# Where V is projected, when K is spread, and when a pair's weights are copied, in an attention and expert kernel

## The chip, the cores and the metric

The kernel runs on one core of a Trainium2 chip. The metric is the time of one execution on the device in microseconds (us). Lower is better.

## The reference

64 sequences of 64 tokens with 256 features (4096 tokens) pass through four steps; everything is fp32.

```python
c  = x @ cond_weight[id] + cond_bias[id]           # per sequence, one of 16 matrices
q, k, v, o projections: c @ W.T + b + c @ A.T @ B.T / 8      # 16 heads of 16
scores = q @ k.T / 4 + slope[h] * (key - query)
x  = x + (c + rezero * o_projection(softmax(scores) @ v))
y  = lora_out[lang](x) + lang_embed[lang]          # rank 16, one of 4 languages
x  = x + geglu(y @ Ws1 + bs1) @ Ws2 + bs2          # shared
       + sum over the top 2 of 12 experts of gate * (geglu(y @ We1 + be1) @ We2 + be2)
```

y has rank 16 in each of 4 languages. So the kernel never forms y: it multiplies the language matrices into the first layers ("merge") and feeds these with the low-rank rows.

## The kernel before

The tokens are cut into 32 tiles of 128 (two sequences each). The order of work is written out by hand for each engine. Engines meet through semaphores: an instruction ends with `then_inc(name)`, another engine executes `wait_ge(name, count)` and everything queued behind that on this engine waits too. Three stages follow each other.

**Attention, tiles 0 to 31 (to about 336 us).** In its tile step i TensorE does, in this order: score(i), c_transpose(i+1), inverse_transpose(i-1), low_rank(i-2) (rank-16 rows of a finished tile), project_k and project_q (i+1), output(i-1), the transpose of the probabilities prob_transpose(i), row_transpose(i-2), x2_transpose(i-1), project_v(i+1), condition(i+2), and last attend(i). VectorE does shift(i) (maximum and subtraction in two halves, with normalize(i-1) between them), k_spread(i+1), t_mask(i-2), x2_add(i-1), half of the copy of the transposed probabilities (pT_copy), sums(i), v_spread(i+1), invert(i), logit_sum(i-2), lang_part(i-1), c_add(i+2). ScalarE copies cT (L564), applies exp to both halves (L577), adds q's bias (L569), and copies transposes. GpSimd adds residuals and cuts merged biases into three bf16 parts.

[...] The scores take columns 0 to 255 of banks 0 to 3, and K and V of the next tile share bank 4: K in columns 0 to 255, V in 256 to 511. [...]

**Merging.** Tiles 1 and 2 merge the shared layer's weights. Tiles 3 to 7 merge nothing. From tile 8 on each expert takes two tiles. The even tile has merge_pair: the weights of two units into bank 6 (merge_weights, L1328), then attend, then their biases into bank 7 (merge_biases, L1334); only behind the biases does merge_ps rise. ScalarE copies the biases at once (pair_bias_copy, L556), and the weights in the odd tile behind the copies of cT and of the inverses (pair_copy, L559). The odd tile merges one unit (merge). low_rank needs bank 6, and so waits for pair_copy (merge_sb); in the odd tile (`after_pair`) it therefore runs behind project_q, in all other tiles ahead of project_k.

**Start.** VectorE adds the low-rank products to the weights of K, Q and V (low_rank_weight, L748) as they land by DMA, with c_add(0), the scaling of two biases, k_spread(0), v_spread(0) and c_add(1) between. SyncE issues the loads; ali_f (the alibi rows) raises the same semaphore as two biases (d_near). Behind tile 0, VectorE does router_consts, lang_part(0) and the rows that mark each sequence's language.

**Shared layer (336 to 446 us)**, in 16 units of 256 tokens: TensorE's hidden (L1454, L1459), gelu on ScalarE, multiply on VectorE (L1035), TensorE's shared_out (L1470), then combine on VectorE (L1045) which frees shared_out's bank (comb_ok). VectorE also ranks the tokens' experts here: expert_bases, slot_bases, slots (L976, L977), slot_parts, gates, then hot_batch (L993 to L1005), on which TensorE's row_ids (L1514) wait.

**Routed experts (446 to 809 us)**: 75 tiles of gathered rows (L1553, L1559, L1572), results added to DRAM by GpSimd (L504).

Of the kernel before, what the change touches and what calls it, by code (L numbers as in the profile page):

```python
# [5 lines left out]
P = 128  # L6
B, S, D = 64, 64, 256
H, HD = 16, 16
# [34 lines left out]
def adaln_attn_moe(nc, args, out):  # L43
# [7 lines left out]
    with ctx:  # L51
# [44 lines left out]
        class Cut:  # L96
# [114 lines left out]
        d_cat, d_first, d_near, d_rest, d_low, d_first_x, d_bs2, d_zero = [sem(n) for n in (  # L211
            "d_cat", "d_first", "d_near", "d_rest", "d_low", "d_first_x", "d_bs2", "d_zero")]
# [24 lines left out]
        merge_ps, merge_sb, pair_bias, r_gap, r_exp, r_chosen, r_rank, r_slots, r_gates, r_done = [sem(n) for n in (  # L237
            "merge_ps", "merge_sb", "pair_bias", "r_gap", "r_exp", "r_chosen", "r_rank", "r_slots", "r_gates", "r_done")]
# [16 lines left out]
        FIRST, NEAR, REST = 16 * 2, 16 * (len(near_loads) + 1), 16 * len(rest_loads)  # L255
# [22 lines left out]
        def _(sp):  # L278
# [37 lines left out]
            sp.dma_start(ali_f, a["alibi"]).then_inc(d_near, 16)  # L316
# [219 lines left out]
        def _(act):  # L536
# [21 lines left out]
            def pair_copy(e):  # L558
                copy(w1m[:, ds(e * (NJ * CW), 2 * CW)], ps[:, 6, 0:2 * CW]).then_inc(merge_sb, 1)  # L559
# [55 lines left out]
            def tile_steps(i, pair_of=None, merged=None, between=lambda: None, idle=lambda: None):  # L615
# [5 lines left out]
                if pair_of is not None:  # L621
                    pair_copy(pair_of)
# [26 lines left out]
            with act.Fori(0, NE - 1) as e:  # L649
                i = 2 * e + MERGE_FROM  # L650
                tile_steps(i)
                pair_bias_copy(e)
                tile_steps(i + 1, pair_of=e, merged=third(e))
            tile_steps(NT - 2, idle=lambda: [unit_copy(u, u) for u in range(2)])
            pair_bias_copy(NE - 1)
# [9 lines left out]
            pair_copy(NE - 1)  # L665
# [68 lines left out]
        def _(dve):  # L734
# [38 lines left out]
            def v_spread(i, odd):  # L773
                dve.wait_ge(v_ps, i + 1)
                for h in range(2):
# [3 lines left out]
                        ps[r, 4, D:2 * D].rearrange("p (b h d) -> p b h d", b=2, d=HD),  # L779
# [105 lines left out]

            def tile_steps(i, odd, between=lambda: None):
                one_more, two_more = not isinstance(i, int) or i + 1 < NT, not isinstance(i, int) or i + 2 < NT
                shift(i)
                if one_more:
                    k_spread(i + 1)  # L890
                between()
                if not isinstance(i, int) or i > 1:
                    t_mask(i - 2)
                if not isinstance(i, int) or i > 0:
                    x2_add(i - 1, not odd)
                pT_copy(i)
# [10 lines left out]
            low_rank_weight(0, PROJECTIONS[0])  # L907
            c_add(0, False)
# [798 lines left out]
```

## Time and profile before

| | before |
|---|---|
| median of three runs | 811.55 us (811.1 to 811.58) |
| the profiled execution | 811.48 us |
| its span | 809.6 us |
| TensorE matmul busy | 787.7 us (97%) |
| TensorE weight load busy | 658.8 us (81%) |
| VectorE busy | 569.6 us (70%) |
| ScalarE busy | 296.0 us (37%) |
| GpSimd busy | 405.5 us (50%) |
| granted TensorE clock | 1.00 of full speed to 443 us, 0.99 behind it |

Times are microseconds from the beginning of the span. PE is TensorE's matmuls, PEld its weight loads (they run beside matmuls), DVE VectorE, ACT ScalarE. L1229 is line 1229 of the kernel. A timeline row gives start, duration, engine, line, operation, output and input by the program's names, and how many instructions are taken together; in brackets stands how long the engine was idle before, and what ended that. "issue" is idle time for which the profile shows no releaser. The ends of matmuls are modelled. In the names, most tensors of the attention stage are slices of "arena"; "ps" is PSUM.

### The profile page before, as it was taken

What the parts mean: (1) busy time and instruction counts of PE and PEld (TensorE: products, weight loads), DVE (VectorE), ACT (ScalarE), POOL (GpSimd) and SP (SyncE); (2) the same over time, 40 slices, a digit from 0 to 9 for tenths busy, and PEclk for the clock granted to TensorE, in tenths of its full rate; (3) what the DMA queues carried; (4) which work ended last, traced back from release to release, by engine and by line L of the source; (5) the groups of instructions that cost most, each with busy time, mean ns of one, the idle gap of its engine ahead of it and who ended that gap; (6) DMA issues with size and microseconds to landing.
All of it is one profiled execution on the core that took longest, in us unless ns stands there. A gap on an engine that the chain in (4) does not pass through costs nothing. (4 is left out here: it accounts for less than half of the span.)

```text
span 809.6 us, 27702 instructions
## 1 busy us (share of the span) xinstructions
PE 787.7 (97%) x9379; PEld 658.8 (81%) x9380; DVE 569.6 (70%) x1350; ACT 296.0 (37%) x883; POOL 405.5 (50%) x511
## 2 busy tenths in 40 slices
PE   8999999999999999999999999999999999999994
PEld 6788888888888888777777888888888888888883
DVE  3889877777777777679884666665666666666662
ACT  1354444444444444532222333333333333333330
POOL 3133244444444444501003677777777777777762
PEclk9999999999999999999999999999999999999998
DMA  8553455565565554046743222322232232223222
GB/s 278 159 176 106 124 165 175 172 179 170 177 181 181 180 180 141 6 144 222 220 157 128 39 35 36 39 36 34 34 39 35 34 35 39 34 33 40 36 30 27
DMA packets 49325, 86.11 MB, mean 106 GB/s; under 512 B 7298, under 2 KB 27970, under 8 KB 49122
## 3 DMA queue, kind: packets, MB, share of 16 engines
q1 hardware_dynamic: 33778, 68.83, 26.7%
q0 software_dynamic: 13888, 15.13, 13.7%
q10 hardware_dynamic: 1584, 1.10, 0.5%
q8 instruction: 54, 0.88, 0.5%
q14 instruction: 21, 0.17, 0.1%
HBM read 68.48 MB, written 16.55 MB: 105 GB/s over the span
## 5 line engine op out<-in xcount | busy, mean ns | idle before, releaser
L1572 PE MATMUL ps<-arena,stage 128*128 x900 | 206.6, 379 | 0.0
L1572 PEld LDWEIGHTS ps<-arena,stage 128*128 128x128 f32 x900 | 165.2, 190 | 19.5
L504 POOL DMA_INDIRECT out_dram<-stage,to_row x75 | 120.7, 1609 | 74.6 <-DVE stage L1139 62.4
L708 ACT ACTIVATE stage<-ps 128x384 f32<-128x384 f32 x150 | 65.4, 488 | 241.6 <-PE ps L1559 238.4
L1559 PE MATMUL ps<-token_rows,token_rows_T 64*128 64x128 f32 x1800 | 129.1, 272 | 0.0
L1559 PEld LDWEIGHTS ps<-token_rows,token_rows_T 64*128 64x128 f32 x1800 | 118.7, 188 | 1.7
L496 POOL DMA_INDIRECT token_rows<-gated_rows,from_row x75 | 75.3, 1004 | 62.6 <-DVE to_row L1018 39.9
L1113 DVE COPY token_rows<-ps 128x128 f32<-128x128 f32 x75 | 21.9, 292 | 115.4 <-PE ps L1541 111.3
L408 POOL TENSOR_TENSOR arena<-arena 128x256 f32<-128x256 f32 x32 | 23.4, 731 | 150.7 <-DVE arena L831 139.9
L794 DVE TENSOR_REDUCE arena<-ps 128x8 f32<-128x512 f32 x64 | 43.9, 686 | 49.3 <-PE ps L1266 48.7
L1123 DVE TENSOR_TENSOR stage<-ps,stage 128x384 f32<-128x384 f32 x150 | 75.9, 548 | 1.8 <-ACT stage L708 1.8
L1229 PE MATMUL ps<-arena 128*128 128x128 f32 x512 | 64.0, 278 | 3.6 <-ACT arena L564 3.6
L1229 PEld LDWEIGHTS ps<-arena 128*128 128x128 f32 x512 | 59.6, 191 | 6.6 <-issue 6.6
L1553 PE MATMUL ps<-token_rows,token_rows_T 64*128 64x256 bf16 x450 | 62.1, 273 | 0.0
L1470 PE MATMUL ps<-ws,stage 128*128 128x256 f32 x256 | 59.1, 384 | 1.4 <-DVE arena L1045 1.4
L577 ACT ACTIVATE arena<-arena 128x512 f32<-128x512 f32 x64 | 40.4, 631 | 44.9 <-DVE arena L796 43.9
L1470 PEld LDWEIGHTS ps<-ws,stage 128*128 128x128 f32 x256 | 47.4, 190 | 11.2 <-issue 5.4
L796 DVE TENSOR_TENSOR arena<-ps,arena 128x512 f32<-128x512 f32 x64 | 44.3, 692 | 2.2
L1115 DVE TENSOR_SCALAR token_rows<-ps,consts 128x128 bf16<-128x128 f32 x150 | 45.0, 342 | 0.0
L1130 DVE TENSOR_SCALAR token_rows_T<-be_bc,token_rows 128x256 f32 x75 | 38.3, 511 | 6.8 <-issue 5.6
L511 POOL COPY token_rows_T<-w_bias 128x384 bf16 x75 | 42.5, 567 | 0.9 <-issue 0.7
L1553 PEld LDWEIGHTS ps<-token_rows,token_rows_T 64*128 64x128 bf16 x450 | 22.2, 96 | 24.9 <-issue 23.2
(173 smaller groups left out, 1468.0 us busy)
## 6 DMA issues: line engine op xcount, KB each, us to landing
stage<-in_we_dram SPq DMA_DIRECT2D x36, 512.0 KB, 4.5
arena<-in_cond_w_dram SPq DMA_DIRECT2D x64, 256.0 KB
arena<-in_we_dram SPq DMA_DIRECT2D x12, 768.0 KB, 5.6
arena<-in_x_both_dram SPq DMA_DIRECT2D x31, 256.0 KB, 2.7
arena<-in_L_cond_bias_dram SPq DMA_DIRECT2D x64, 64.0 KB, 2.9
out_dram<-arena SPq DMA_DIRECT2D x32, 128.0 KB, 2.2
be_bc<-in_be_rows_dram SPq DMA_DIRECT2D x13, 192.0 KB, 3.3
gated_rows<-token_rows POOLq DMA_DIRECT2D x2, 1152.0 KB, 10.9
```

What stands on the lines that cost most here:

```text
L496: pool.indirect_dma_start(s_row[s], None, gated_rows, bass.IndirectOffsetOnAxis(from_row[:, t:t + 1], 0)).then_inc(d_row[s], 16)
L504: pool.indirect_dma_start(out_rows, bass.IndirectOffsetOnAxis(to_row[:, t:t + 1], 0), y_sb[t % YR], None, compute_op=ALU.add).then_inc(d_a ...
L708: nc.scalar.activation(g_sb[hf].rearrange("p (j n) -> p j n", n=P), first_out[1][:, :, hf, :], ACT.Gelu).then_inc(g_ok, 1)
L794: V.tensor_reduce(top, scores[:, banks], AX.X, ALU.max).then_inc(max_sb, 1)
L796: V.tensor_tensor(probs[:, 512 * half:512 * half + 512].rearrange("p (g h k) -> p g h k", g=2, k=S), scores[:, banks], top.unsqueeze(3).to ...
L1115: last = V.tensor_scalar(s_langT[s % 2][:, hf * P:(hf + 1) * P], ps[:, 7, P:2 * P], col["half"][:, hf:hf + 1], None, ALU.mult)
L1123: V.tensor_tensor(actT_sb[s % 2][:, hf, :].rearrange("p (j n) -> p j n", n=P), first_out[0][:, :, hf, :], g_sb[hf].rearrange("p (j n) -> p ...
L1229: last = mm(ps[:, bank, at + m * P:at + (m + 1) * P], wm[w][:, k, m * P:(m + 1) * P], cT[:, k, :], start=(k == 0), stop=(k == KC - 1))
L1470: last = mm(ps[:, 4 + v, half * D:(half + 1) * D], sh_aT[half][:, k, v * P:(v + 1) * P], ws2[:, k, :], start=(k == 0), stop=(k == HS // P ...
L1553: mm(first_out[g][:, j].rearrange("p h n -> p (h n)"), w1bx[s % 2].bitcast(bf16)[64 * g:64 * g + 64, at], s_langT[s % 2][64 * g:64 * g + 6 ...
L1559: last = mm(first_out[g][:, j, hf, :], w1x[s % 2][64 * g:64 * g + 64, j * CW + hf * P:j * CW + (hf + 1) * P], s_rowT[s % 2][64 * g:64 * g ...
L1572: last = mm(ps[:, 4 + s % 2, 0:D], actT_sb[s % 2][:, hf, j * P:(j + 1) * P], arena[:, ds(e * E2 + (NJ * hf + j) * D, D)], start=(hf == 0 a ...
```

## The change

V of tiles 1 to 31 is projected into columns 0 to 255 of bank 2, one of the scores' banks, and V of tile 0 into bank 6, instead of bank 4. project_v then waits for nothing of K, and project_k for nothing of V; score(i) waits for v_sb in their place. On VectorE, k_spread goes behind t_mask and x2_add. merge_pair raises a new semaphore pair_ps behind its weights, ScalarE runs pair_copy at the end of the even tile behind that, and low_rank goes ahead of project_k in odd tiles too. At the start the order of VectorE's list changes, ali_f gets its own semaphore, the router's rows go into tile 1 and the language rows behind tile 2. In the shared layer, combine(2) goes ahead of the slot sums.

```diff
...
@@ -252,7 +252,7 @@
...
             (a_rows, a["lora_a"]), (aT.rearrange("p c l n -> p (c l n)"), a["lora_aT"])]
-        FIRST, NEAR, REST = 16 * 2, 16 * (len(near_loads) + 1), 16 * len(rest_loads)
+        FIRST, NEAR, REST = 16 * 2, 16 * len(near_loads), 16 * len(rest_loads)
         PROJECTIONS = (1, 0, 2, 3)
@@ -313,7 +313,7 @@
...
             sp.dma_start(wm[n].rearrange("p c n -> p (c n)"), a["wT"][n]).then_inc(d_wT[n], 16)
-            sp.dma_start(ali_f, a["alibi"]).then_inc(d_near, 16)
+            sp.dma_start(ali_f, a["alibi"]).then_inc(d_ali, 16)
             n = PROJECTIONS[2]
@@ -556,6 +556,7 @@
...
             def pair_copy(e):
+                act.wait_ge(pair_ps, e + 1)
                 copy(w1m[:, ds(e * (NJ * CW), 2 * CW)], ps[:, 6, 0:2 * CW]).then_inc(merge_sb, 1)
@@ -612,14 +613,12 @@
...
-            def tile_steps(i, pair_of=None, merged=None, between=lambda: None, idle=lambda: None):
+            def tile_steps(i, merged=None, between=lambda: None, idle=lambda: None):
                 one_more = not isinstance(i, int) or i + 1 < NT
...
                     invT_copy(i - 1)
-                if pair_of is not None:
-                    pair_copy(pair_of)
                 exps(i)
@@ -649,9 +648,11 @@
...
                 tile_steps(i)
+                pair_copy(e)
                 pair_bias_copy(e)
-                tile_steps(i + 1, pair_of=e, merged=third(e))
+                tile_steps(i + 1, merged=third(e))
             tile_steps(NT - 2, idle=lambda: [unit_copy(u, u) for u in range(2)])
+            pair_copy(NE - 1)
             pair_bias_copy(NE - 1)
@@ -662,7 +663,6 @@
...
-            pair_copy(NE - 1)
             invT_copy(NT - 2)
@@ -772,11 +772,12 @@
...
                 dve.wait_ge(v_ps, i + 1)
+                values = ps[:, 6, D:2 * D] if isinstance(i, int) and i == 0 else ps[:, 2, 0:D]
                 for h in range(2):
...
                         vD[int(odd)][r, :, :, h * HD:(h + 1) * HD],
-                        ps[r, 4, D:2 * D].rearrange("p (b h d) -> p b h d", b=2, d=HD),
+                        values[r, :].rearrange("p (b h d) -> p b h d", b=2, d=HD),
                         bv_half[r, :].rearrange("p (h d) -> p h d", d=HD).unsqueeze(1).to_broadcast([S, 2, 8, HD]),
@@ -883,16 +884,21 @@
...
+            def router_setup():
+                router_consts()
+                dve.wait_ge(ar_sb, 1)
+                lang_part(0)
+
             def tile_steps(i, odd, between=lambda: None):
...
                 shift(i)
+                if not isinstance(i, int) or i > 1:
+                    t_mask(i - 2)
+                if not isinstance(i, int) or i > 0:
+                    x2_add(i - 1, not odd)
+                between()
                 if one_more:
                     k_spread(i + 1)
-                between()
-                if not isinstance(i, int) or i > 1:
-                    t_mask(i - 2)
-                if not isinstance(i, int) or i > 0:
-                    x2_add(i - 1, not odd)
                 pT_copy(i)
@@ -905,27 +911,25 @@
...
             low_rank_weight(0, PROJECTIONS[0])
+            dve.wait_ge(d_first, FIRST)
+            V.tensor_scalar(bq_quarter, bq_col, 0.25, None, ALU.mult).then_inc(s_first, 1)
+            dve.wait_ge(d_near, NEAR)
+            V.tensor_scalar(bo_rz, bo_bc, rz, None, ALU.mult).then_inc(s_first, 1)
             c_add(0, False)
             low_rank_weight(1, PROJECTIONS[1])
-            dve.wait_ge(d_first, FIRST)
-            V.tensor_scalar(bq_quarter, bq_col, 0.25, None, ALU.mult).then_inc(s_first, 1)
+            low_rank_weight(2, PROJECTIONS[2])
             k_spread(0)
-            low_rank_weight(2, PROJECTIONS[2])
-            dve.wait_ge(d_near, NEAR)
+            dve.wait_ge(d_ali, 16)
             V.tensor_copy(ali, ali_f).then_inc(s_const, 1)
-            V.tensor_scalar(bo_rz, bo_bc, rz, None, ALU.mult).then_inc(s_first, 1)
+            c_add(1, True)
             dve.wait_ge(s_zero, 3)
             v_spread(0, False)
-            c_add(1, True)
             tile_steps(0, False, lang_setup)
-            router_consts()
-            dve.wait_ge(ar_sb, 1)
-            lang_part(0)
+            tile_steps(1, True, router_setup)
+            tile_steps(2, False)
             link(V.tensor_scalar(lang_tmp, lang_tmp, col["lang_row"], col["one_row"], ALU.is_equal, ALU.add))
...
                 V.tensor_scalar(langB[:, hf, :], lang_tmp, col["half"][:, hf:hf + 1], None, ALU.mult)
-            tile_steps(1, True)
-            tile_steps(2, False)
             with dve.Fori(0, NE) as e:
@@ -1071,10 +1075,10 @@
...
             slot_bases()
+            for v in range(2):
+                combine(2, v, 0)
             slots(0, r_m1)
             slots(1, r_m2)
-            for v in range(2):
-                combine(2, v, 0)
             slot_parts()
@@ -1180,6 +1184,7 @@
...
                 pe.wait_ge(d_rest, REST)
+                pe.wait_ge(v_sb, 1)
                 for c in range(KC):
@@ -1231,20 +1236,18 @@
...
             def project_k(i):
-                if not isinstance(i, int) or i > 0:
-                    pe.wait_ge(v_sb, i)
                 transposed(1, 4, 0, tile=i).then_inc(k_ps, 1)
...
             def project_v(i):
-                pe.wait_ge(k_sb, i + 1)
+                out = ps[:, 6, D:2 * D] if isinstance(i, int) and i == 0 else ps[:, 2, 0:D]
                 wv = [wm[2][:, k, :].rearrange("p (h two d) -> p two h d", two=2, d=HD) for k in range(KC)]
...
                         for k in range(KC):
-                            last = mm(ps[h * S:(h + 1) * S, 4, D + b * P:D + (b + 1) * P].rearrange(
+                            last = mm(out[h * S:(h + 1) * S, b * P:(b + 1) * P].rearrange(
                                 "p (h d) -> p h d", d=HD), cT[:, k, b * S:(b + 1) * S], wv[k][:, h],
@@ -1255,6 +1258,7 @@
...
                     pe.wait_ge(pTv_sb, i)
+                    pe.wait_ge(v_sb, i + 1)
                 for b in range(2):
@@ -1325,8 +1329,9 @@
...
                     for g in range(2):
-                        mm(ps[64 * g:64 * g + 64, bank, at:at + CW].rearrange("p (h n) -> p h n", h=2), ba[:, c, 0:NLR],
+                        last = mm(ps[64 * g:64 * g + 64, bank, at:at + CW].rearrange("p (h n) -> p h n", h=2), ba[:, c, 0:NLR],
                            stage_w[j][:, c, 2 * g:2 * g + 2, :], start=(c == 0), stop=(c == KC - 1))
+                return last
@@ -1354,7 +1359,8 @@
...
                 for j in range(2):
-                    merge_weights(j, j * CW)
+                    last = merge_weights(j, j * CW)
+                last.then_inc(pair_ps, 1)
                 inside()
@@ -1371,13 +1377,11 @@
...
                     inverse_transpose(i - 1)
-                if late and after_pair is None:
+                if late:
                     low_rank(i - 2, merged)
...
                     project_q(i + 1)
-                if late and after_pair is not None:
-                    low_rank(i - 2, merged)
                 between()
@@ -1431,7 +1435,6 @@
...
             pe.wait_ge(d_stage[2], 16 * NE)
-            pe.wait_ge(v_sb, NT)
             merge_weights(2, 0, bank=4)
...
             output(NT - 2)
```

## Rows read from the trace of the kernel before

**Rows 1.** Timeline of a plain tile (tile 6 to 7), TensorE and VectorE
```profile
73.11 0.69 DVE L794 TENSOR_REDUCE arena<-ps 128x8 f32<-128x512 f32 x1
73.11 0.44 PE L1221 MATMUL ps<-consts,arena 128*128 128x128 f32 x2 [0.26 <-DVE arena L762]
...
75.86 1.03 PE L1302 MATMUL ps<-arena 128*128 128x256 f32 x4
76.09 0.87 DVE L767 SCALAR_TENSOR_TENSOR arena<-ps,arena,consts 128x256 f32<-128x256 f32 x2
...
77.19 0.41 DVE L831 TENSOR_TENSOR arena<-ps,arena 128x256 f32<-128x256 f32 x1
...
81.83 0.69 DVE L794 TENSOR_REDUCE arena<-ps 128x8 f32<-128x512 f32 x1 [0.15 <-issue]
```

**Rows 2.** Timeline of tiles 0 and 1
```profile
16.39 1.09 PE L1214 MATMUL ps<-arena 128*64 128x256 f32 x8 [0.56 <-issue]
...
17.51 0.42 DVE L762 TENSOR_TENSOR arena<-ps,arena 128x256 f32<-128x256 f32 x1 [0.72 <-PE ps L1214]
...
18.29 0.69 DVE L794 TENSOR_REDUCE arena<-ps 128x8 f32<-128x512 f32 x1 [0.35 <-PE ps L1266]
...
26.80 0.42 DVE L762 TENSOR_TENSOR arena<-ps,arena 128x256 f32<-128x256 f32 x1
...
28.34 0.69 DVE L794 TENSOR_REDUCE arena<-ps 128x8 f32<-128x512 f32 x1
...
32.13 0.66 PE L1275 MATMUL ps<-consts,arena 128*128 128x128 f32 x4 [0.42 <-ACT arena L577]
```

**Rows 3.** Timeline of the shared layer
```profile
366.81 3.69 PE L1470 MATMUL ps<-ws,stage 128*128 128x256 f32 x16 [1.41 <-DVE arena L1045]
...
375.04 0.78 DVE L1005 TENSOR_TENSOR hot_id<-hot_tile,consts 128x600 bf16<-128x600 f32 x1
...
376.26 0.70 PE L1514 MATMUL ps<-hot_id,hot_position 128*128 128x150 bf16 x8
```

**Rows 4.** Timeline of an odd merge tile (low_rank behind K and Q)
```profile
205.30 0.32 PE L1260 MATMUL ps<-arena 2*64 2x256 bf16 x8
...
206.91 2.02 PE L1229 MATMUL ps<-arena 128*128 128x128 f32 x16 [0.23 <-ACT arena L564]
...
209.20 1.04 PE L1302 MATMUL ps<-arena 128*128 128x256 f32 x4
210.08 1.04 PE L1275 MATMUL ps<-consts,arena 128*128 128x128 f32 x8
...
211.06 0.38 PE L1308 MATMUL ps<-consts,arena 128*128 128x128 f32 x2
...
212.89 0.85 DVE L777 TENSOR_TENSOR arena<-ps,arena 64x256 f32<-64x256 f32 x2
```

**Rows 5.** Timeline of the even merge tile behind it (low_rank ahead)
```profile
215.20 0.32 PE L1260 MATMUL ps<-arena 2*64 2x256 bf16 x8
...
218.67 1.03 PE L1302 MATMUL ps<-arena 128*128 128x256 f32 x4
...
219.53 1.15 PE L1275 MATMUL ps<-consts,arena 128*128 128x128 f32 x8
...
220.32 0.41 DVE L831 TENSOR_TENSOR arena<-ps,arena 128x256 f32<-128x256 f32 x1
...
220.79 0.44 PE L1308 MATMUL ps<-consts,arena 128*128 128x128 f32 x2
```

**Rows 6.** Waits of PE, 40 to 310 us; who L1308 waits for
```profile
PE ps L1229 <- ACT arena L564: 2.3, 10, 0.2
...
  DVE arena L831: 2.7, 14
```

**Rows 7.** Waits of L1247 (project_v), and a wait at L1334
```profile
  issue: 5.2, 31
...
334.21 0.38 PEld L1334 LDWEIGHTS ps<-stage,ba 128*32 128x32 f32 x16 [0.17 <-issue]
```

More of the change, by code:

```diff
@@ L207, in adaln_attn_moe @@
             "p (j h n) -> p j h n", h=2, n=P) for g in range(2)]
-        d_cat, d_first, d_near, d_rest, d_low, d_first_x, d_bs2, d_zero = [sem(n) for n in (
-            "d_cat", "d_first", "d_near", "d_rest", "d_low", "d_first_x", "d_bs2", "d_zero")]
+        d_cat, d_first, d_near, d_ali, d_rest, d_low, d_first_x, d_bs2, d_zero = [sem(n) for n in (
+            "d_cat", "d_first", "d_near", "d_ali", "d_rest", "d_low", "d_first_x", "d_bs2", "d_zero")]
         d_wT = [sem(f"d_wT{c}") for c in "qkvo"]
@@ L236, in adaln_attn_moe @@
         tile_hot, ids_hot, ids_ps, ids_sb = sem("tile_hot"), sem("ids_hot"), sem("ids_ps"), sem("ids_sb")
-        merge_ps, merge_sb, pair_bias, r_gap, r_exp, r_chosen, r_rank, r_slots, r_gates, r_done = [sem(n) for n in (
-            "merge_ps", "merge_sb", "pair_bias", "r_gap", "r_exp", "r_chosen", "r_rank", "r_slots", "r_gates", "r_done")]
+        merge_ps, merge_sb, pair_ps, pair_bias, r_gap, r_exp, r_chosen, r_rank, r_slots, r_gates, r_done = [sem(n) for n in (
+            "merge_ps", "merge_sb", "pair_ps", "pair_bias", "r_gap", "r_exp", "r_chosen", "r_rank", "r_slots", "r_gates", "r_done")]
         d_row = [sem(f"d_row{s}") for s in range(RING)]
@@ L888, in tile_steps @@
                 shift(i)
-                if one_more:
-                    k_spread(i + 1)
-                between()
                 if not isinstance(i, int) or i > 1:
@@ L895, in tile_steps @@
                     x2_add(i - 1, not odd)
+                between()
+                if one_more:
+                    k_spread(i + 1)
                 pT_copy(i)
```

## The prediction

> **What bounds the kernel now.** I read the share of each engine over the whole run first, then the waits by engine, and then the timeline of one tile in each regime. TensorE is busy for 787.7 of 809.6 us (the table), so almost any change in time must come out of its small gaps, or be put into them. A busy TensorE in this profile is not TensorE at its peak, since the ends of its matmuls are modelled; so I compare *starts* of the same groups in two tiles, which are not. The granted clock was 1.00 wherever the change works (the table), so no clock term enters.
>
> The attention stage has three regimes. Tiles 8 to 30 also merge expert weights ("merge tiles"; an odd one takes 215.20 - 205.30 = 9.9 us [rows 4, 5]); there TensorE sets the pace and VectorE waits for it. Tiles 3 to 7 merge nothing ("plain tiles"); there VectorE has no pause, and TensorE waits for its last operation: the c_transpose at 73.11 us waits 0.26 us for the c_add (L762) [rows 1]. Tiles 0 and 1 hang on DMA and then on a long VectorE list [rows 2]. Behind the attention one long wait of TensorE is left, 1.41 us [rows 3].
>
> **Merge tiles: low_rank goes ahead of K and Q in odd tiles.** In an odd merge tile TensorE waits 0.23 us at L1229 for ScalarE's copy of cT (L564) [rows 4], and only behind K and Q does low_rank run. In an even one low_rank already stands in front and fills that wait. From the score's first matmul to output (L1302): odd 209.20 - 205.30 = 3.90 us [rows 4], even 218.67 - 215.20 = 3.47 us [rows 5]. The change makes the odd tile like the even one: 0.43 us less, more than the 0.23 us shown, since the modelled end hides part of the gap. Its condition is that pair_copy is done before low_rank: ScalarE now runs it right behind merge_weights of the even tile, waiting for the new signal pair_ps. In that place ScalarE is idle, and only pair_bias_copy is queued behind it, which waits for a later event (merge_ps) anyway. So pair_copy costs nothing where it goes. Not all 0.43 us stay: the second half of the probabilities' transpose waits for the second exp, whose time after the score does not change. The even tile shows this: from L1275's start to x2_transpose's (L1308) it takes 220.79 - 219.53 = 1.26 us against 211.06 - 210.08 = 0.98 us, and the transposes themselves appear as 1.15 us instead of 1.04 [rows 4, 5]. I split the 0.28 us into 0.12 for the exp and 0.16 for x2_add, by that 0.11. Net for an odd tile: 0.43 - 0.12 = 0.31 us. L1229 waited for the copy 10 times in the window that I read, one such tile being outside it [rows 6]; the code has 11 such tiles: 11 x 0.31 = 3.4 us. Bounds: 0 (the exp takes it all) and 11 x 0.43 = 4.7 us.
>
> **Merge tiles: K is spread after x2_add.** In the even tile x2_add (L831) starts at 220.32, 0.62 us after output's modelled end (218.67 + 1.03 = 219.70), as k_spread and t_mask stand before it; L1308 then waits [rows 5]. With k_spread behind it, x2_add is ready long before the transposes end, and the 0.16 us go. L1308 waited 14 times for it [rows 6]; 11 of these I put in even merge tiles: 11 x 0.16 = 1.8 us (bounds 0.8 and 2.7, half of my value and the whole of the row). k_spread delays all that follows on VectorE by 0.2 to 0.4 us. Who waits? attend, which comes behind project_v, condition and the merged weights; and the next score, which now waits for v_sb too, since V lies in its bank 2. V's spread ended at 212.89 + 0.85 = 213.74, the next score began at 215.20 [rows 4, 5]; 1.46 us of slack shrink by 0.43 and by 0.4 at most. Cost zero.
>
> **project_v loses its wait for k_sb.** L1247 shows "issue" of 0.17 us before it in every tile, 5.2 us over 31 [rows 7]. Is this the wait? merge_biases at 334.21 (L1334) follows 128-column transposes with *no* wait in the code and has the same 0.17 us [rows 7]. The gap goes with the change of the tile shape, which stays. I count 0; the other end is -0.17 us in each of 27 tiles = -4.6 us, and is a rival below. [...]
>
> **Plain tiles: a pause moves into VectorE.** This is what the change costs. Count from c_transpose at 73.11, where VectorE's shift starts too. output starts at 75.86, its modelled end is 76.89, and a vector instruction follows such an end by some 0.03 us (16.39 + 1.09 = 17.48 against 17.51 [rows 2]); so x2_add can start at 76.92, or +3.81. Shift is over at 76.09; with k_spread's 0.87 us taken out, x2_add's turn comes at 77.19 - 0.87 = 76.32 [rows 1]. k_spread used to lie in just this time; now VectorE stands idle for 0.5 to 0.6 us. As VectorE is the bound and TensorE's c_transpose waits for its last operation, TensorE cannot run ahead. A period is 81.83 - 73.11 = 8.72 us here; it holds small waits of VectorE, of which the row at 81.83 shows 0.15, and such waits vanish where a longer one stands ahead of them. I take 0.6 less 0.27: some 0.33 net for each of five tiles, a period of about 9.0, 1.6 us lost (bounds 0 and 5 x 0.6 = 3.0).
>
> **Start.** Condition 1 (L1214, 16.39) had waited 0.56 us for its weights by DMA, and c_add(1) ends at 17.93 in both orders [rows 2]. Earlier values, scalings and the moved K spread save nothing there, as no DMA is moved. But v_spread(0), which was hidden behind that DMA wait, now follows c_add(1): 17.93 + 0.86 = 18.79, so shift(0) starts 0.5 us later than 18.29. The extra half microsecond runs down VectorE's list to the next score, which waits for v_sb (+0.65 us on TensorE). In exchange router_consts, lang_part and the language rows (1.12 us between the end of c_add(2), 26.80 + 0.42, and shift(1) at 28.34 [rows 2]) leave that place: shift(1) comes at about 28.1. TensorE's last wait in tile 1 is for the exp that follows shift(1) (0.42 us at 32.13 [rows 2]), so it goes by that: -0.14 us at the beginning of tile 2 (bounds -1.0 and +1.0). The language rows go behind tile 2, a tile that merges, where VectorE has slack: free (0.8 us at most if it had none). x2_add's wait in tile 2 gives 0.1.
>
> **Behind the attention.** combine(2) goes ahead of the two slot sums. shared_out(3) at 366.81 waited for it 1.41 us [rows 3]. That goes, but TensorE then comes early to the second row_ids, whose hot ids end at 375.04 + 0.78 = 375.82; the two batches start at 376.26 and take 0.70 [rows 3], so the second began at about 376.6. VectorE moves up by some 0.4 us only (a combine that no longer waits, an earlier gelu), and so the second batch could start at 375.4 + 0.2. Gain 1.0 us (bounds 0.5 and 1.5).
>
> **Sum.** -3.4 - 1.8 + 1.6 - 0.14 - 0.1 - 1.0 = -4.9 us. The profiled execution took 811.48 us (span 809.6 and 1.9 around it), the median is 811.55: 806.7.
>
> **Rivals.**
> 1. *The project_v gap was the wait.* -4.6 more: 802.1. For: it is there in all 31 tiles. Against: the row without a wait.
> 2. *The exps take the gains.* If ScalarE's second exp is what TensorE meets in both kinds of merge tile, odd tiles give 0 and even ones half (0.9), and the plain tiles lose their upper 3.0: 811.5 - 0.9 + 3.0 - 1.2 = 812.4 at worst, 811 with the likely 1.6: no change that can be told. For: the even tile already meets the exp. Against: by 0.12 us only.
> 3. *Slower: V's spread holds the next score in the merge tiles.* Score now waits for v_sb, and VectorE reaches v_spread only behind x2_add's wait. It decides from where x2_add's release comes 0.6 us later than I reckon (the slack of 1.46 less 0.83). If it came 0.9 late, 27 tiles from 3 on would lose 0.3 each, 8.1 us: 806.7 + 8.1 = 814.8. Against: the release at 17.51 follows its modelled end by 0.03 us [rows 2].
>
> **How the numbers follow.** Forecast 806.7, own range 804 to 809.5, chance 0.72; rival 1 0.08, rival 2 0.12, rival 3 0.08. The range of 803.0 to 810.0 reaches towards rivals 1 and 2 and leaves rival 3 out. 0.2% (1.6 us) is about what a measurement of this kernel can tell from no change. Faster by more: the forecast and rival 1, 0.80; within: 0.11; slower: 0.09.
>
> **What would show it.** Right: no wait of L1229 for the copy, odd tiles of 9.6 us; no waits of L1308 in merge tiles; a new VectorE wait of 0.5 us before L831 for output in plain tiles, with periods of 9.0 us; L1247 still with 0.17 us; shift(0) at 18.8; shared_out(3) directly behind hidden, and a short wait before row_ids. Wrong: merge tiles of unchanged length, a wait of the score for V's spread, or plain tiles as short as before.

## The result, and the profile after

| | before | after |
|---|---|---|
| median | 811.57 us (811.1 to 811.66, 4 runs) | 805.25 us (804.97 to 806.17, 4 runs) |
| ratio to before | | 0.9927 [0.9915, 0.9939] |
| the profiled execution, its span | 811.48 us, 809.6 | 806.17 us, 804.4 |
| TensorE matmul busy | 787.7 us | 783.6 us |
| VectorE busy | 569.6 us | 575.9 us |

The change gives 6.3 us; the forecast was 4.9 (806.7, range 803.0 to 810.0). Its direction and its mechanisms hold, and most of the difference lies in two terms. Line numbers in after are 3 to 5 higher: c_transpose is L1226, project_v L1250, output L1306, prob_transpose L1279, x2_transpose L1312, low_rank L1321, x2_add L832, the two spreads L767 and L778, the shift L795 and L797.

I measured both traces in starts of TensorE's groups, stretch by stretch. "Score to score" is the distance between the first matmuls of L1264 in two tiles.

| stretch | before | after | difference | forecast |
|---|---|---|---|---|
| condition(0) to score(2) | 28.18 | 27.78 | -0.40 | -0.14 |
| score(2) to score(3) | 9.63 | 9.54 | -0.09 | -0.1 |
| score(3) to score(8), plain tiles | 42.87 | 43.73 | +0.86 | +1.6 |
| score(8) to score(31), merge tiles | 240.76 | 235.22 | -5.54 | -5.2 |
| score(31) to the last shared_out | 112.60 | 111.03 | -1.57 | -1.0 |

Of the last line, 0.47 us is chance: one shared unit took 6.67 us instead of 6.21 in the profiled execution of before, and with the same order of combine in two experiments (e3, e4 below) it took 6.21. Without that the line is -1.10, and the sum is -0.40 - 0.09 + 0.86 - 5.54 - 1.10 = -6.27 us; the medians differ by 6.32. That they agree so closely is in part luck. The spans differ by 5.2 only: in this execution of after, condition(0) began 0.54 us later, and from the last shared_out to the end, where nothing was changed, it took 368.0 us against 367.0. This last stretch takes 366.5 to 369.1 us in the profiled executions of all the kernels here, so differences of the whole time below a microsecond or two are better read from the stretches.

**Merge tiles.** Timeline of after, both engines: first an even tile (pair), then an odd one.

```profile
193.01 0.32 PE L1264 MATMUL ps<-arena 2*64 2x256 bf16 x8
...
196.47 1.03 PE L1306 MATMUL ps<-arena 128*128 128x256 f32 x4
...
197.33 1.23 PE L1279 MATMUL ps<-consts,arena 128*128 128x128 f32 x8
197.53 0.42 DVE L832 TENSOR_TENSOR arena<-ps,arena 128x256 f32<-128x256 f32 x1
...
198.50 0.38 PE L1312 MATMUL ps<-consts,arena 128*128 128x128 f32 x2
...
203.94 0.32 PE L1264 MATMUL ps<-arena 2*64 2x256 bf16 x8
...
205.00 0.69 DVE L795 TENSOR_REDUCE arena<-ps 128x8 f32<-128x512 f32 x1 [2.47 <-PE ps L1270]
...
205.16 0.60 PE L1321 MATMUL ps<-arena 128*128 128x112 f32 x4
...
205.59 1.96 PE L1234 MATMUL ps<-arena 128*128 128x128 f32 x16
...
207.39 1.03 PE L1306 MATMUL ps<-arena 128*128 128x256 f32 x4
...
208.25 1.18 PE L1279 MATMUL ps<-consts,arena 128*128 128x128 f32 x8
208.46 0.42 DVE L832 TENSOR_TENSOR arena<-ps,arena 128x256 f32<-128x256 f32 x1
...
208.80 0.87 DVE L767 SCALAR_TENSOR_TENSOR arena<-ps,arena,consts 128x256 f32<-128x256 f32 x2
...
211.31 0.84 DVE L778 TENSOR_TENSOR arena<-ps,arena 64x256 f32<-64x256 f32 x2
...
213.52 0.32 PE L1264 MATMUL ps<-arena 2*64 2x256 bf16 x8
```

The odd tile takes 213.52 - 203.94 = 9.58 us (9.90 before, [rows 4, 5]). low_rank (205.16) stands ahead of K and Q (205.59), which have no bracket: nobody waits for cT. Score to output is 207.39 - 203.94 = 3.45 us, like the even tile's 3.46. The even tile's x2_add starts at 197.53, 0.03 us behind output's modelled end (196.47 + 1.03 = 197.50); before, it was 0.62 us [rows 5]. V's spread ends at 211.31 + 0.84 = 212.15, 1.37 us ahead of the next score: nothing of rival 3. What the transposes still meet is the exp, as the waits between 40 and 310 us show (engine, waiting line and releaser: us, times, longest):

```profile
PEld ps L1279 <- ACT arena L578: 3.5, 19, 0.2
DVE arena L832 <- PE ps L1306: 2.8, 8, 0.5
```

No wait of L1312 for x2_add is left in the list [rows 6]. The second line counts VectorE's waits before x2_add, in tiles 2, 4 to 8, 27 and 28; most of it is the pause in the plain tiles.

**Plain tiles.** Timeline of after, tile 6 and the c_transpose of the next tile:

```profile
72.50 0.32 PE L1264 MATMUL ps<-arena 2*64 2x256 bf16 x8 [0.15 <-DVE arena L778]
...
73.71 0.44 PE L1226 MATMUL ps<-consts,arena 128*128 128x128 f32 x2 [0.42 <-DVE arena L762]
...
76.44 1.03 PE L1306 MATMUL ps<-arena 128*128 128x256 f32 x4
...
77.50 0.42 DVE L832 TENSOR_TENSOR arena<-ps,arena 128x256 f32<-128x256 f32 x1 [0.46 <-PE ps L1306]
77.85 0.86 DVE L767 SCALAR_TENSOR_TENSOR arena<-ps,arena,consts 128x256 f32<-128x256 f32 x2
...
78.63 0.68 DVE L805 COPY arena<-ps 128x512 f32<-128x512 f32 x1
...
82.55 0.44 PE L1226 MATMUL ps<-consts,arena 128*128 128x128 f32 x2 [0.41 <-DVE arena L762]
```

VectorE now has the foretold pause before x2_add (0.46 us), and TensorE waits longer for its c_add: 0.42 us against 0.26 [rows 1]. The period is 82.55 - 73.71 = 8.84 us. The score itself waits 0.15 us for V's spread (L778, row at 72.50), as rival 3 had it, but only in tiles 1 and 5 to 8, and c_transpose waits for VectorE again right behind it. pT_copy at 78.63 follows without a wait; with K spread early it waits 0.16 us there (e1), one of the small waits that the new one takes in.

**Start.** Timeline of after to tile 2: TensorE, then VectorE, then TensorE with ScalarE's second exp of tile 1 (everything 0.54 us late by the first DMA):

```profile
9.13 1.09 PE L1219 MATMUL ps<-arena 128*64 128x256 f32 x8 [0.51 <-DMA arena<-in_cond_w_dram]
...
16.94 1.09 PE L1219 MATMUL ps<-arena 128*64 128x256 f32 x8 [1.30 <-issue]
```
```profile
18.07 0.42 DVE L762 TENSOR_TENSOR arena<-ps,arena 128x256 f32<-128x256 f32 x1 [2.63 <-PE ps L1219]
18.41 0.84 DVE L778 TENSOR_TENSOR arena<-ps,arena 64x256 f32<-64x256 f32 x2
19.29 0.69 DVE L795 TENSOR_REDUCE arena<-ps 128x8 f32<-128x512 f32 x1
...
28.50 0.69 DVE L795 TENSOR_REDUCE arena<-ps 128x8 f32<-128x512 f32 x1 [0.28 <-PE ps L1270]
```
```profile
27.63 0.32 PE L1264 MATMUL ps<-arena 2*64 2x256 bf16 x8 [0.36 <-DVE arena L778]
...
31.60 0.63 ACT L578 ACTIVATE arena<-arena 128x512 f32<-128x512 f32 x1 [1.02 <-DVE arena L797]
31.90 1.04 PE L1279 MATMUL ps<-consts,arena 128*128 128x128 f32 x8
...
36.91 0.32 PE L1264 MATMUL ps<-arena 2*64 2x256 bf16 x8
```

The second exp and score(2) in before:

```profile
31.44 0.63 ACT L577 ACTIVATE arena<-arena 128x512 f32<-128x512 f32 x1 [1.02 <-DVE arena L796]
...
36.77 0.32 PE L1260 MATMUL ps<-arena 2*64 2x256 bf16 x8
```

shift(0) begins 19.29 - 16.94 = 2.35 us behind condition 1, before 18.29 - 16.39 = 1.90 [rows 2]: 0.45 us later. The wait for the exp in tile 1 (0.42 us, [rows 2]) is no longer shown, and the score waits 0.36 us for V instead. Yet TensorE still goes by that exp: score(2) begins 36.91 - 31.60 = 5.31 us behind it, before 36.77 - 31.44 = 5.33. From score(0) to score(2) it takes 18.95 us, before 19.36. The other runs with after's start show 18.94 to 18.96 (e1, e2, e3, e6, e7, e12), and e4, with the start of before, 19.36.

**Shared layer.** TensorE in after:

```profile
360.69 3.72 PE L1473 MATMUL ps<-ws,stage 128*128 128x256 f32 x16
...
370.19 0.43 PE L1517 MATMUL ps<-hot_id,hot_position 128*128 128x150 bf16 x4
370.78 0.44 PE L1517 MATMUL ps<-hot_id,hot_position 128*128 128x150 bf16 x4 [0.15 <-DVE hot_id L1009]
```

shared_out(3) follows hidden directly (1.41 us of waiting before, [rows 3]); of what it wins, the second row_ids gives back a part by its short wait.

### The profile page after: what moved, and what is told of

It reads as the page before. It is cut to its first block, busy times and chain, and to the rows that moved or that the text cites. A ratio compares the mean times of both kernels' runs of the same rounds, so it can differ in the third digit from the quotient of the medians.

```text
span 804.4 us, 27682 instructions
## 1 busy us (share of the span) xinstructions
PE 783.6 (97%) x9379; PEld 658.2 (82%) x9380; DVE 575.9 (72%) x1350; ACT 294.3 (37%) x883; POOL 405.4 (50%) x511
## 4 chain that ended last, share of the span: by engine, by line
PE 90%; DVE 5%; issue 2%; DMA 1%; SPq 0%; POOL 0%; ACT 0%; DVEq 0%
PE ps L1575 24%; PE ps L1562 13%; PE ps L1234 7%; PE ps L1473 6%; PE ps L1332 4%; PE ps L1556 4%; PE ps L1306 3%; PE ps L1250 3%; PE ps L1279 3%; PE ps L1462 3%; PE ps L1219 3%; PE ps L1543 2%; PE ps L1339 2%; PE ps L1292 2%; PE ps L1321 2%
## 5 line engine op out<-in xcount | busy, mean ns | idle before, releaser
L795 DVE TENSOR_REDUCE arena<-ps 128x8 f32<-128x512 f32 x64 | 43.9, 686 | 42.4 <-PE ps L1270 42.0
L797 DVE TENSOR_TENSOR arena<-ps,arena 128x512 f32<-128x512 f32 x64 | 44.3, 691 | 2.2
L270 DVE COPY token_rows_T<-w_merged 128x256 f32 x75 | 44.7, 596 | 0.7 <-issue 0.7
L590 ACT COPY arena<-arena 128x128 f32<-128x128 f32 x64 | 15.9, 295 | 73.4 <-DVE arena L817 73.4
```

Source lines behind the costliest of these rows:

```text
L270: copy(w1x[s % 2][:, j * CW:(j + 1) * CW], w1m[:, ds(e * (NJ * CW) + j * CW, CW)]).then_inc(w1x_ok[j], 1)
L797: V.tensor_tensor(probs[:, 512 * half:512 * half + 512].rearrange("p (g h k) -> p g h k", g=2, k=S), scores[:, banks], top.unsqueeze(3).to ...
```

## The experiments

In each, "after" is the changed kernel, and the times of before lie between 811.1 and 811.5 in the same sets.

**e1: after, with K spread early again.**

```diff
                 shift(i)
+                if one_more and True:
+                    k_spread(i + 1)
                 if not isinstance(i, int) or i > 1:
                     t_mask(i - 2)
...
                 between()
-                if one_more:
+                if one_more and not (True):
                     k_spread(i + 1)
                 pT_copy(i)
```

> The changed kernel with one thing undone: k_spread stands directly behind shift again, ahead of t_mask and x2_add, in all tiles. My theory (late K frees x2_transpose in the merge tiles and puts a pause of VectorE into the plain ones): the plain tiles lose their pause and fall from 8.84 us to 8.6 or less (-1.0 us for five), while x2_add comes late again in the merge tiles, 0.16 us in each even one and about 0.2 in each odd one, 11 of each (+4.0): in sum +3.0 over the changed kernel's 805.25, so 808.2 us. Rival (the place of the K spread is of no account, the gain came with the bank): 805.3. Rival (the plain tiles' pause is the larger term): 804.3.

Measured: 809.21 us, 0.9974 [0.9963, 0.9986]. Plain tiles 8.56 us on average, score(3) to score(8) 42.79 (-0.94 against after); odd merge tiles 9.80 (+0.22), even ones 11.09 (+0.15), score(8) to score(31) 239.29 (+4.07). Its waits between 40 and 310 us:

```profile
PEld ps L1314 <- DVE arena L832: 4.4, 23, 0.2
```

The wait for x2_add is back, and 23 times instead of 13 in the same window of before (14 in the whole run, [rows 6]): once low_rank is ahead, odd tiles meet it too. So K's late place buys some 4.1 us in the merge tiles and costs 0.9 in the plain ones. It also shows that the terms depend on each other: low_rank's move without K's gives an odd tile 9.90 - 9.80 = 0.10 us only, and 0.07 of that is the bank's (e4).

**e2: after, with low_rank behind K and Q in the odd merge tiles.**

```diff
-                if late:
+                if late and after_pair is None:
                     low_rank(i - 2, merged)
                 if one_more:
                     project_k(i + 1)
                     project_q(i + 1)
+                if late and after_pair is not None:
+                    low_rank(i - 2, merged)
```

> The changed kernel with low_rank behind project_q again in the 11 odd merge tiles; pair_copy stays in its new place. My theory: each odd tile grows from 9.57 us to about 9.9 (0.43 less the 0.12 that the second exp had taken back), +3.4 us in all, so 808.7 us, and TensorE waits 0.23 us for the copy of cT in these tiles again. Rival (the early pair_copy alone relieves ScalarE, the place of low_rank is of no account): 805.3.

Measured: 809.10 us, 0.9973 [0.9962, 0.9983]. Odd tiles 9.84 us (+0.26), score(8) to score(31) 237.95 (+2.7). The wait for the copy of cT is back in ten tiles of the window:

```profile
PEld ps L1234 <- ACT arena L565: 3.7, 10, 0.4
```

The median is 3.9 us above after's and this stretch accounts for 2.7 (see "What stays open").

**e3: after, with combine(2) behind the slot sums again.**

```diff
-            for v in range(2):
-                combine(2, v, 0)
             slots(0, r_m1)
             slots(1, r_m2)
+            for v in range(2):
+                combine(2, v, 0)
```

> The changed kernel with combine(2) behind the two slot sums again. My theory: shared_out(3) waits 1.4 us again and row_ids waits no longer: +1.0 to +1.1 us, 806.3 us. Rival (all 1.4 us came through and 0.4 us more in the rest of the shared layer hang on it): +1.5 to +1.9, 807.0 us.

Measured: 807.20 us, 0.9949 [0.9931, 0.9967]; by the trace, score(31) to the last shared_out is 112.14 instead of 111.03 (+1.1).

```profile
362.32 3.69 PE L1473 MATMUL ps<-ws,stage 128*128 128x256 f32 x16 [1.42 <-DVE arena L1049]
```

The wait is there again with its old length, and 1.1 of its 1.42 us reach the end. The median says 1.95.

**e4: before, with only V moved to the scores' bank** (and the waits that belong to it).

```diff
             def project_k(i):
-                if not isinstance(i, int) or i > 0:
-                    pe.wait_ge(v_sb, i)
...
             def project_v(i):
-                pe.wait_ge(k_sb, i + 1)
+                out = ps[:, 6, D:2 * D] if isinstance(i, int) and i == 0 else ps[:, 2, 0:D]
...
                     pe.wait_ge(pTv_sb, i)
+                    pe.wait_ge(v_sb, i + 1)
```

> The kernel before with one part of the change alone: V of tiles 1 to 31 is projected into the scores' bank 2 (tile 0: bank 6), project_v no longer waits for k_sb nor project_k for v_sb, the score waits for v_sb. All orders are the old ones. My theory (the 0.17 us before project_v belong to the change of tile shape, and no other wait was for these two signals): no change, 811.6 us within 0.8. Rival 1 of the prediction (the gap was the wait): -4.6 us, 807.0 us.

Measured: 811.40 us, 1.0001 [0.999, 1.0011]. Score(8) to score(31) is 240.07, 0.69 us less than before, with odd tiles 0.06 shorter. The waits that the other parts remove are all still there:

```profile
PEld ps L1231 <- ACT arena L564: 3.7, 10, 0.4
PEld ps L1309 <- DVE arena L832: 2.5, 13, 0.2
```

So rival 1 falls. In before, project_v waits for k_sb (K is spread) and project_k for v_sb (V of the tile before is spread). With project_v's wait for K gone, the time of the kernel stays, and so does the gap: in e4 and in after the view of project_v's line gives the same as before [rows 7]:

```profile
  issue: 5.2, 31
```

No wait is left there. What makes the gap no run separates. In the weight loads of before it stands ahead of project_v (0.17 us at 211.37 and at 221.16), where tiles of 64 columns follow tiles of 128, and not ahead of condition (212.19, 221.98) and of the merged weights (212.95, 222.73), where 64 follow 64; that it comes of the change of the tile is inferred from that and from the row at 334.21 [rows 7]. The bank's move is worth next to nothing itself (the ratio is 1.0001); it takes project_v's wait for k_sb away, and so K can be spread late.

**e5: after, with v_spread(0) ahead of c_add(1)**, under condition 1's wait for its weights.

```diff
-            c_add(1, True)
             dve.wait_ge(s_zero, 3)
             v_spread(0, False)
+            c_add(1, True)
```

> The changed kernel with v_spread(0) ahead of c_add(1) again, so behind TensorE's wait for the weights of condition 1. My theory: shift(0) starts 0.5 us sooner after c_add(1), score(1) loses its wait for v_sb (0.36 us) and the time falls by 0.3 to 0.5 us: 804.85, too small for the clock of a run but plain in the trace. Rival (TensorE meets a DMA or an exp in tile 1 that eats it): 805.25, and score(1) at the same distance from condition 1.

Measured: 805.08 us, 0.9923 [0.9909, 0.9936]. Timeline of VectorE:

```profile
16.21 0.86 DVE L778 TENSOR_TENSOR arena<-ps,arena 64x256 f32<-64x256 f32 x2
18.08 0.42 DVE L762 TENSOR_TENSOR arena<-ps,arena 128x256 f32<-128x256 f32 x1 [1.01 <-PE ps L1219]
18.86 0.69 DVE L795 TENSOR_REDUCE arena<-ps 128x8 f32<-128x512 f32 x1 [0.35 <-PE ps L1270]
```

The first period is 9.22 us instead of 9.67. This is the half microsecond that the change had put behind c_add(1). In the whole time 0.45 us is within the spread of the runs.

**e6: after, with K early in tiles 3 to 7 and late in all others.** VectorE's loop had to be split for it, so tiles 3 to 7 are also written out one by one, and tiles 27 to 29, which after has written out, run in the loop: two edits in one.

```diff
                 shift(i)
+                if one_more and isinstance(i, int) and 2 < i < MERGE_FROM:
+                    k_spread(i + 1)
...
-            with dve.Fori(0, NE) as e:
-                tile_steps(2 * e + 3, True)
-                tile_steps(2 * e + 4, False)
-            for i in range(2 * NE + 3, NT):
+            for i in range(3, MERGE_FROM):
+                tile_steps(i, i % 2 == 1)
+            with dve.Fori(0, NE - 1) as e:
+                tile_steps(2 * e + MERGE_FROM, False)
+                tile_steps(2 * e + MERGE_FROM + 1, True)
+            for i in range(NT - 2, NT):
                 tile_steps(i, i % 2 == 1)
```

> The changed kernel with k_spread directly behind shift in the five plain tiles 3 to 7 only, and behind x2_add in all others. My theory: VectorE's pause of 0.46 us before x2_add goes in these tiles, their period falls from 8.84 to about 8.6 us, and the time by 1.0 us: 804.2. If the score's wait for v_sb were what lengthened them, and not the pause: 805.25.

Measured: 804.24 us, 0.9907 [0.9891, 0.9922]. Plain tiles 8.33 to 8.44 us, score(3) to score(8) 41.84 (-1.89). K's place gives 0.94 of that by e1; the other 0.95 I put to the writing out, which I had not expected (alone, in e12, it gives 0.71). The merge tiles keep their 9.57 and 10.96, and tiles 27 to 29, now looped, take these times too, where after has 9.43 and 10.73.

**e7: after, with row_transpose between the halves of prob_transpose**, to fill the wait for the second exp.

```diff
-                prob_transpose(i)
+                prob_transpose(i, range(4))
                 if late:
                     row_transpose(i - 2)
+                prob_transpose(i, range(4, 8))
```

> The changed kernel with row_transpose(i-2) moved between the two halves of the probabilities' transpose in every tile. It needs neither exp. My theory (TensorE meets the second exp in both kinds of merge tile, by 0.12 to 0.18 us): the transpose fills this wait, 23 tiles by 0.12 (what it can cover, its own length being 0.11): -2.5 us, 802.8. Rival (the stretched 1.18 us of the eight transposes are only how their ends are modelled): 805.25.

Measured: 803.48 us, 0.9903 [0.9888, 0.9918]. Odd 9.47, even 10.76 (after 9.58 and 10.94), score(8) to score(31) 232.87 (-2.35). So in both kinds of merge tile the second exp was the last thing that held TensorE: the piece of rival 2 that is true, and it is worth 0.1 to 0.2 us a tile.

**e8: e5, e6 and e7 together.**

> The changed kernel with the three edits together: v_spread(0) ahead of c_add(1), k_spread early in tiles 3 to 7 only, row_transpose between the halves. My theory: the terms add, -0.4 - 1.0 - 2.5 = -3.9 us, 801.4 us. If one of them takes the cover of another, less: down to the best of them alone.

Measured: 802.35 us, 0.9895 [0.988, 0.991]: the gain is about a microsecond smaller than expected. The plain tiles take about 8.74 us instead of e6's 8.33 to 8.44, and score(3) to score(8) 43.58 instead of 41.84. TensorE in a plain tile of e8, and then of e6:

```profile
76.17 0.60 PE L1283 MATMUL ps<-consts,arena 128*128 128x128 f32 x4
76.75 0.33 PE L1331 MATMUL ps<-consts,arena 128*128 128x128 f32 x1
76.91 0.60 PE L1283 MATMUL ps<-consts,arena 128*128 128x128 f32 x4
77.35 0.38 PE L1316 MATMUL ps<-consts,arena 128*128 128x128 f32 x2
```
```profile
75.87 1.04 PE L1283 MATMUL ps<-consts,arena 128*128 128x128 f32 x8
...
76.85 0.38 PE L1316 MATMUL ps<-consts,arena 128*128 128x128 f32 x2
```

From the first transpose to x2_transpose it is 1.18 us against 0.98. row_transpose needs VectorE's t_mask, which the early K pushes back in just these tiles. VectorE, the bound there, then waits longer for the transposes (0.53 us against 0.22 in e6):

```profile
77.55 0.69 DVE L805 COPY arena<-ps 128x512 f32<-128x512 f32 x1 [0.53 <-PE ps L1283]
```

**e9: after, with an extra vector instruction of half K's spread behind the real one**, its result unused. It tests how much slack V's spread has.

```diff
                 if one_more:
                     k_spread(i + 1)
+                    k_again()
                 pT_copy(i)
```

> The changed kernel with one more half K spread (0.47 us on VectorE, into a tile that nobody reads) behind the real one in every tile. My theory (TensorE sets the pace in merge tiles, where V's spread ends 1.37 us or more before the score that waits for it; VectorE sets it in plain tiles): merge tiles keep 9.58 and 10.94 us, plain tiles grow by the full 0.4 to 0.47 each: +2.2 us, and +0.4 at the start: 807.8. The slower rival of the prediction (the score's new wait for V's spread is near the bound everywhere): all 28 tiles grow by 0.45, +12 us, 817.

Measured: 809.12 us, 0.9976 [0.9966, 0.9985] (10 runs). Timeline of VectorE in a plain tile:

```profile
82.36 0.86 DVE L768 SCALAR_TENSOR_TENSOR arena<-ps,arena,consts 128x256 f32<-128x256 f32 x2
83.14 0.47 DVE L775 SCALAR_TENSOR_TENSOR x_spare<-ps,arena,consts 128x256 f32<-128x256 f32 x1
```

The extra instruction takes 0.39 us of VectorE's time (83.14 to the next start at 83.53). Each plain period is longer by that, 9.23 instead of 8.84, +1.97 in all; score(8) to score(31) is 235.28, as in after (235.22). So the merge tiles have the slack that I reckoned, and rival 3 is out. The other 1.9 of the 3.9 us that the median lost are not placed. Ahead of score(3) this execution lost 3.6 us, but its start was also held up by a late transfer and by the clock (last section), and behind the attention it was faster than that of after.

**e12: after, with VectorE's loop over tiles 3 to 26 written out.** No order changes.

```diff
-            with dve.Fori(0, NE) as e:
-                tile_steps(2 * e + 3, True)
-                tile_steps(2 * e + 4, False)
-            for i in range(2 * NE + 3, NT):
+            for i in range(3, NT):
                 tile_steps(i, i % 2 == 1)
```

> The changed kernel with VectorE's loop over tiles 3 to 26 written out, the same instructions in the same order. In the changed kernel's trace, shift begins 1.11 us after the score in looped tiles and 0.88 us in those that are written out (tile 29), and the last tiles take 10.73 and 9.44 us where looped ones take 10.94 and 9.58. My theory (waits against a register's value wake VectorE about 0.2 us later, and TensorE meets that in the second exp): merge tiles fall to 10.73 and 9.44 us, 18 looped ones by 0.17 on average, -3.1 us; the plain ones by up to 0.15 each: 801.8 us. Rival (the last tiles are shorter for another reason, their place at the end): 805.25.

Measured: 801.97 us, 0.9888 [0.9873, 0.9902]. Odd 9.43, even 10.73, plain 8.67; score(8) to score(31) 232.02 (-3.2). TensorE and VectorE of e12:

```profile
200.47 0.32 PE L1261 MATMUL ps<-arena 2*64 2x256 bf16 x8
```
```profile
201.35 0.69 DVE L795 TENSOR_REDUCE arena<-ps 128x8 f32<-128x512 f32 x1 [2.28 <-PE ps L1267]
```

The shift begins 0.88 us behind the score; in the looped tiles of after it is 205.00 - 203.94 = 1.06. Tile 29 of after, which is written out there already, has 0.88 too (315.53 and 316.41):

```profile
316.41 0.69 DVE L795 TENSOR_REDUCE arena<-ps 128x8 f32<-128x512 f32 x1 [0.98 <-PE ps L1270]
```

The second exp comes by that much earlier, and TensorE's transposes no longer meet it.

**e11 and e13: the parts together, with row_transpose between the halves only where tiles merge.** e11 is e5 + e6 + this; e13 has in addition all of VectorE's loop written out.

> The kernel with the three edits, but row_transpose stays behind both halves in the plain tiles, where it waits for a t_mask that the early K spread delays (their period was 8.74 us with it between, 8.42 without). My theory: plain tiles 8.42, merge tiles 9.47 and 10.76 us, start as with v_spread(0) first: 805.25 - 1.9 - 2.35 - 0.45 = 800.6 us. Rival (the plain tiles' loss had another source): 802.3.

> As the kernel before this one in the list, with VectorE's loop over the tiles written out entirely. My theory (row_transpose between the halves already covers the second exp in the merge tiles, so writing the loop out finds nothing left to give): the same within 0.6 us, 800.5 us. If register waits cost TensorE anything besides the exp: up to 3 us less, 797.5.

Measured: e11 800.44 us, 0.9863 [0.9849, 0.9877]; e13 800.24 us, 0.9866 [0.9851, 0.988]. Plain tiles take 8.33 to 8.43 us in both: e8's loss is gone, so its cause is shown: row_transpose between the halves in the plain tiles. Merge tiles take 9.46 and 10.77 in e11, 9.43 and 10.73 in e13. Writing out and filling the wait cover the same gap and do not add: once one is there, the other gives 0.03 us a tile. Both are faster than after by some 5 us, and than before by 11.

## Why the prediction was right

The terms of my sum add up to -4.84 us, not -4.9; the time of 806.7 goes with 4.84. Against it the stretches show -6.27, and the plain tiles (0.74), the merge tiles (0.34) and the start (0.26) make the difference.

**Merge tiles (forecast -5.2, measured -5.54).** Comparing the same groups in an odd and an even tile gave 0.31 us for an odd one and 0.16 for an even one; the periods fell by 0.32 and 0.15. The split of 0.28 us into 0.12 for the exp and 0.16 for x2_add, which I had put down with little behind it, fits within 0.01 us, but in part by luck. low_rank's place is worth 0.26 us in an odd tile (e2) and not 0.31, and only with K late (e1). Another 0.07 comes with the bank (e4), a term that I had put at nothing: project_k starts 1.51 us behind the score there, before 1.61 (206.91 - 205.30, [rows 4]). It did not wait for V's spread, which had long ended (in tile 21 of before at 223.30 us, with project_k at 227.89); why the start moved is not shown. The excess over 5.2 lies mostly in tiles 27 and 29, which are written out: there the second exp comes earlier, and each became 0.46 us shorter.

**Plain tiles (+1.6, measured +0.86).** The mechanism was right and the size off. Score to score, the five tiles take 8.50, 8.50, 8.66, 8.49 and 8.72 us in before and 8.36, 8.85, 8.84, 8.84 and 8.84 in after. So four tiles lost 0.25 us each, where 0.33 was forecast for five, and tile 3, which has no pause, gained 0.14. My period of 8.72 was the longest of unequal ones. In the pause itself, I took k_spread out with its duration of 0.87 us, but its place in the list is 78.63 - 77.85 = 0.78 from start to start; that alone makes the pause about 0.1 us shorter. I also took the upper end (0.6) of my own estimate of 0.5 to 0.6, where the row shows 0.46, and odd tiles have only 0.3. The part that is not lost takes the place of small waits that VectorE had anyway, as reckoned.

**Start (-0.14, measured -0.40).** The mechanism was right here too: shift(0) is 0.45 us later, the first period grew by 0.68 us (forecast 0.65), and score(2) follows shift(1) at the same distance, 8.41 us in after and 8.43 in before. The term was mis-sized twice. shift(1) was to come at 28.1 and came at 28.50, less the 0.54 by which this execution ran late: 27.96, which is 0.38 ahead of before's 28.34. And of the 0.24 us that my own 28.1 gave, I put only 0.14 into the sum, without a reason.

**Shared layer (-1.0, measured -1.10).** Both halves are in the trace: the wait of 1.41 us gone, and a new short one (0.15) before the second row_ids. e3 gives the same 1.1 from the other side.

**The rivals.** 1: excluded by e4 and by the unchanged 5.2 us over 31 tiles: 0.17 us a tile stays where no wait is. The forecast's 0 for this term rests on the row at 334.21 [rows 7] alone; what makes the gap is not shown. 2: true for one small part, the second exp's hold (e7, e12: 2.35 and 3.2 us could still be had), wrong as a limit. 3: excluded by e9, where V's spread comes 0.39 us later still and no merge tile gets longer.

**What stays open.** By their medians e1, e2 and e3 lose 0.8 to 1.2 us more than the stretches account for. Against the profiled execution of after (806.17 us) they do not: 809.02, 809.07 and 807.42 are 2.9, 2.9 and 1.3 us more, and their stretches with the start give the same. It is after whose profiled execution lies 0.9 us above its median. A slower chip is not the reason, as before took 811.14 us (29 runs) on the chip of e1 to e3. What makes the untouched last stretch differ by over 1 us between executions is open. Why a looped tile's shift starts later is not shown either, only that it does (1.05 to 1.13 us behind the score against 0.88).

## What to carry to other kernels

Where two kinds of tile differ by one order, the distances between the starts of the same groups in both price that order well, as long as what else the change moves is priced too: here the order gave 0.26 us of the forecast 0.31. A place in an engine's list is worth its distance from start to start, not the duration of its row: k_spread's was 0.78 us here, its row 0.87. The same operation can be late in one stage and early in another: K's spread belongs behind x2_add where TensorE is the bound (-4.1 us) and ahead of it where VectorE is (-0.9 us), and an operation moved into a gap must be checked against what feeds it in every stage (e8: 43.58 us for score(3) to score(8) instead of 41.84).

## What the runs showed of the hardware

**The shift of a looped tile started later.** In after, VectorE's shift (L795) starts 1.05 to 1.13 us after the score's first matmul (L1264) in merge tiles 9 to 26, which VectorE runs in its loop, and 0.88 to 0.89 us after it in tiles 27 to 31, which are written out; before has 1.04 to 1.06 us in tiles 8 to 26 and 0.88 to 0.89 in tiles 27 to 31. It holds in both directions: e12 writes tiles 3 to 26 out, and tiles 9 to 26 show 0.88 to 0.89; e6 loops tiles 27 to 29, and they show 1.05 to 1.15. In the loop the counts of the waits are worked out from the loop's index, in the written out tiles they are constants; whether this or something else of the loop makes the difference, which e12's expectation puts to waits against a register, no run separates. TensorE's merge tiles were 0.15 us (9.58 against 9.43) and 0.21 us (10.94 against 10.73) longer with the loop, though VectorE had been idle for 1.1 to 2.5 us ahead of its shift: 3.2 us of 805 (e12).

**The clock at the start.** In the profiled execution of e9 the granted clock was 0.83 between 10 and 20 us and 0.86 between 30 and 42, where after has 1.00. Taken by the microsecond it is 0.50 from 13 to 16 us and 0.50 to 0.51 from 30 to 33. Before the first fall TensorE had stood idle for 1.31 and 0.45 us (for c_add and for the copy of cT), before the second for 0.74 and 0.36. One project_k took 3.55 us instead of 2.02. VectorE's weights landed late as well (2.97 us of waiting for DMA ahead of 15.93 us), but behind the fall. The periods of tiles 0 and 1 were 10.06 us instead of 9.67 and 11.07 instead of 9.28, the extra instruction included. e7's profiled execution has 0.83 between 10 and 20 us too (0.50 to 0.53 from 14 to 17): c_transpose had waited 2.15 us there, and project_k took 2.77 us. In after the same idle times as ahead of e9's first fall were 0.92 and 0.45 us, and the clock stayed at 1.00. It stayed there too in e2 with 1.44 and 0.45 us and in e13 with 1.58 and 0.45, so no run shows that the idle time brought it down.
